# Attention scores on 32 rows a head: key columns without a block diagonal, and transposed scores with batch and key on partitions

## The reference

```python
q, k, v = proj(layernorm(x), Wq, bq), proj(ctx, Wk, bk), proj(ctx, Wv, bv)   # (B, 16, 64, 8)
q, k = _rope(q), _rope(k)
scores = jnp.einsum('bhqd,bhkd->bhqk', q, k) / math.sqrt(hd)
scores = jnp.where(m == 0, NEG_INF, scores)
p_attn = jax.nn.softmax(scores, axis=-1)
x1 = x + tanh(g_xattn) * (merge_heads(einsum('bhqk,bhkd->bhqd', p_attn, v)) @ Wo.T + bo)
# then: every row goes through the one of 8 experts (128 -> 512 -> 128, gelu) that its router picks
out = x1 + tanh(g_ffn) * gate * expert(layernorm(x1))
```

## Time and profile before

| what | value |
|---|---|
| median of three runs | 288.04 us (286.25 to 291.29) |
| the profiled execution | 287.01 us, its span 285.2 us |
| busy over the span | PE 80%, PEld 68%, DVE 66%, POOL 63%, ACT 58% |
| matmul records | 3785 |
| mean granted clock of TensorE | 0.958 of full speed |

### The profile page before, as it was taken

The page is one execution under the profiler, slowest core; times in us unless marked ns, Lnnn a source line. Parts: engine busy times, 40 slices in busy tenths (PEclk is TensorE's granted clock), DMA queues, the critical chain, the costliest instruction groups (busy, mean ns, idle before and its releaser), DMA issues.

```text
span 285.2 us, 11006 instructions
## 1 busy us (share of the span) xinstructions
PE 229.3 (80%) x3785; PEld 193.4 (68%) x3785; DVE 189.1 (66%) x639; ACT 164.9 (58%) x482; POOL 180.3 (63%) x222
## 2 busy tenths in 40 slices
PE   1357888987988987789879896598789899999950
PEld 1245677765866765667768675376689799999950
DVE  4546778788798888988867868886575344444310
ACT  1236669696677886568865886436464344444410
POOL 5366757568467889467896686704877654555550
PEclk9999999999799999979996999979999999999995
DMA  7801466546543673314351221333143443110100
GB/s 216 230 15 28 102 148 169 143 103 144 144 129 79 171 177 67 105 32 126 67 150 37 42 48 34 76 85 86 45 143 91 123 119 79 50 33 24 39 21 0
DMA packets 58537, 26.53 MB, mean 93 GB/s; under 512 B 38608, under 2 KB 53989, under 8 KB 58484
## 3 DMA queue, kind: packets, MB, share of 16 engines
q1 hardware_dynamic: 55204, 20.02, 29.3%
q0 software_dynamic: 2272, 4.46, 4.7%
q10 hardware_dynamic: 1008, 1.35, 1.6%
HBM read 16.57 MB, written 5.51 MB: 77 GB/s over the span
## 4 chain that ended last, share of the span: by engine, by line
PE 43%; DVE 19%; issue 11%; ACT 10%; POOL 5%; DMA 5%; SPq 3%; DVEq 0%; POOLq 0%
PE ps L752 13%; DVE mx L1240 5%; PE ps L771 4%; PE ps L795 4%; PE ps L770 3%; PE ps L733 3%; PE ps L735 3%; PE ps L734 3%; ACT vx L644 2%; DVE qk L1185 2%; SPq L411 2%; ACT kT L630 2%; DMA w_r<-in_W_last_row 2%; ACT qk L616 2%; DMA kbd<-kT 2%
## 5 line engine op out<-in xcount | busy, mean ns | idle before, releaser
L565 POOL DMA_INDIRECT out<-fin,got x39 | 37.9, 971 | 28.2 <-DVE fin L1299 23.4
L1240 DVE TENSOR_REDUCE mx<-ps 128x16 f16<-128x1024 f32 x32 | 39.0, 1219 | 12.8 <-PE ps L813 12.7
L752 PE MATMUL ps<-w_f,hT 128*128 x312 | 44.6, 286 | 0.1
L517 POOL DMA_INDIRECT rows<-x_all,dest_i x32 | 33.3, 1041 | 17.0 <-DVE x_all L1075 9.5
L795 PE MATMUL ps<-vx,pr 128*64 128x32 f32 x1024 | 38.0, 229 | 4.9 <-DVE on L1175 4.0
L795 PEld LDWEIGHTS ps<-vx,pr 128*64 128x64 f32 x1024 | 34.5, 144 | 8.9 <-issue 5.3
L544 POOL TENSOR_TENSOR rot<-qk,cf 128x256 f32<-128x256 f32 x32 | 23.4, 732 | 24.7 <-ACT qk L616 17.6
L752 PEld LDWEIGHTS ps<-w_f,hT 128*128 128x128 f32 x312 | 37.8, 191 | 1.1 <-issue 0.3
L1299 DVE SCALAR_TENSOR_TENSOR fin<-ps,got 128x128 f32<-128x128 f32 x39 | 13.7, 351 | 35.9 <-PE ps L752 35.9
L531 POOL TENSOR_TENSOR stk<-rot,stk 128x256 f16<-128x256 f32 x32 | 21.5, 671 | 20.4 <-DVE stk L1253 20.4
L594 ACT ACTIVATE pr<-ps 128x1024 f32<-128x1024 f32 x32 | 32.7, 1021 | 2.2 <-PE ps L843 1.6
(11 more groups left out here) (158 smaller groups left out, 585.1 us busy)
## 6 DMA issues: line engine op xcount, KB each, us to landing
kbd<-kT SPq DMA_DIRECT2D x128, 32.0 KB, 2.5
got<-rows SPq DMA_DIRECT2D x39, 72.0 KB, 2.0
w_f<-in_W_rows SPq DMA_DIRECT2D x8, 256.0 KB, 2.9
w_r<-in_W_last_row SPq DMA_DIRECT2D x8, 256.0 KB, 3.2
w_f<-in_L_ffn_W SPq DMA_DIRECT2D x8, 256.0 KB, 4.7
x_all<-in_x SPq DMA_DIRECT2D x3, 512.0 KB, 5.2
xt_all<-in_x_t SPq DMA_DIRECT2D x3, 512.0 KB, 4.8
ct_all<-in_ctx SPq DMA_DIRECT2D x3, 512.0 KB, 4.5
```

The costliest lines, as they stand in the source:

```text
L517: pool.indirect_dma_start(out=rows, out_offset=bass.IndirectOffsetOnAxis(ap=dest_i[:, t:t + 1], axis=0), in_=x_all[:, t, :], in_offset=Non ...
L565: pool.indirect_dma_start(out=out_d, out_offset=bass.IndirectOffsetOnAxis(ap=got_i[:, u % GOT, R_ID:R_ID + 1], axis=0), in_=fin[:, u % FRI ...
L752: mm = pe.matmul(o, hT[:, par, c, :], w2_f[:, bass.ds(e, 1), c, :].rearrange("p o n -> p (o n)"), start=False, stop=(c == FC - 1))
L1240: dve.tensor_reduce(mx[:, t % 2, :].rearrange("p (w h) -> p w h", w=2)[:, :, 0:8], ps_s[:, :].rearrange("p (w h k) -> p w h k", w=2, k=S), ...
```

## The change

`kbd` is gone, with its DMAs, its zeroing and its waits. `kT` gets four buffers. Scores are made for each head alone: 32 partitions, 64 query columns as weights, 64 keys moving, 32 products a tile. The transposed scores now have batch and key (64 + 64) on partitions and head by query in columns; each batch and head has one selector product and one product of kT and qT, 32 and 32 a tile. The value products take one head each: 32 fp32 products a tile (of 64 partitions, 64 columns as weights, 9 moving). The values lie in `vx` with batch and key on partitions, so that one ScalarE instruction copies them. Scores and transposed scores are made in two halves, in turn, each half with row blocks w and w + 2 (which write to different PSUM banks); each second half waits for the last product of the first one. Both stand after L825 in the step. SyncE issues the chunk and expert loads in one list. The exponential, the maximum and the copies of kT and qT keep their sizes.

```diff
-        kT = sb("kT", [P, 2, NA, P], F16)
+        kT = sb("kT", [P, RING, NA, P], F16)
-        kbd = sb("kbd", [P, RING, 2 * NA, 2, S], F16)
-        vx = sb("vx", [P, RING, 2, 8, 32])
+        vx = sb("vx", [P, RING, H, 16])
-        pr = sb("pr", [P, 2, 8, 2, S])
+        pr = sb("pr", [P, 2, H, S])
...
# SyncE
-            def step(i):
-                t = i - 1
-                if live(t):
-                    sp.wait_ge(kT_ev, t + 1)
...
-                    for g in range(4):
-                        r = slice(STK * g, STK * g + STK)
-                        sp.dma_start(kbd[r, s, :, g % 2, :],
-                                     kT[r, par, :, :].rearrange("p a (b k) -> p (a b) k", b=2)).then_inc(kbd_ld[s], 16)
...
+            columns_of(2)
+            context_of(2)
+            sp.dma_start(ids[:, :], const_i).then_inc(s_ids, 16)
+            expert_of(0)
+            columns_of(3)
...
+            for e in range(2, NE):
+                expert_of(e)
# GpSimd
-            pool.memset(vx[:, :, :, :, :], 0.0).then_inc(s_vz, 1)
-            pool.memset(kbd[:, 0:2, :, :, :], 0.0).then_inc(s_kz, 1)
# ScalarE
-                    if t >= 2:
-                        act.wait_ge(kbd_ld[(t - 2) % RING], ((t - 2) // RING + 1) * 64)
...
-                    for b in range(2):
-                        for hh in range(2):
-                            act.activation(vx[64 * hh:64 * hh + 64, s, b, :, 16 * hh:16 * hh + HD],
-                                           v_ps[64 * b:64 * b + 64, :, hh, :], ACT.Copy).then_inc(v_ev, 1)
+                    act.activation(vx[:, s, :, 0:HD], ps_kv[:, D:2 * D].rearrange("p (h d) -> p h d", d=HD), ACT.Copy
+                                   ).then_inc(v_ev, 1)
# TensorE
+            def scores(t, half):
+                s = t % RING
+                for a in range(NA):
+                    for b in range(2):
+                        for w in (half, half + 2):
+                            r, c = head_rows(w), (NA * w + a) * S
+                            mm = pe.matmul(ps_s[S * b:S * b + S, c:c + S], qT[r, s, a, S * b:S * b + S],
+                                           kT[r, s, a, S * b:S * b + S], start=True, stop=True)
+                return mm
+            def scores_T(t, half):
+                s = t % RING
+                for a in range(NA):
+                    for b in range(2):
+                        for w in (half, half + 2):
+                            r, c, k = head_rows(w), (NA * w + a) * S, slice(S * b, S * b + S)
+                            pe.matmul(ps_st[k, c:c + S], sel_h[r, a, :], mxT[r, t % 2, k], start=True, stop=False)
+                    for b in range(2):
+                        for w in (half, half + 2):
+                            r, c, k = head_rows(w), (NA * w + a) * S, slice(S * b, S * b + S)
+                            mm = pe.matmul(ps_st[k, c:c + S], kT[r, s, a, k], qT[r, s, a, k], start=False, stop=True)
+                return mm
...
-                    for j in range(8):
+                    for h in range(H):
                         for b in range(2):
-                            mm = pe.matmul(ps_o[S * b:S * b + S, 32 * j:32 * j + 32], pr[:, par, NA * (j % 2) + j // 2, b, :],
-                                           vx[:, s, b, j, :],
-                                           start=True, stop=True)
+                            k = slice(S * b, S * b + S)
+                            mm = pe.matmul(ps_o[k, 16 * h:16 * h + HD + 1], pr[k, par, NA * (h % 4) + h // 4, :],
+                                           vx[k, s, h, 0:HD + 1], start=True, stop=True)
...
-                    for a in range(NA):
-                        for b in range(2):
-                            for w in range(2):
-                                r, c = rows_half(w), (NA * w + a) * P
-                                mm = pe.matmul(ps_s[S * b:S * b + S, c:c + P], qT[r, s, a, S * b:S * b + S],
-                                               kbd[r, s, 2 * a + b, :, :].rearrange("p h k -> p (h k)"),
-                                               start=True, stop=True)
-                    mm.then_inc(s_done, 1)
# after the transpose of on (L825):
+                t = i - 2
+                if live(t):
+                    pe.wait_ge(kT_ev, t + 1)
+                    pe.wait_ge(qT_ev, t + 1)
+                    wait(pe, mx_done, t)
+                    scores(t, 0).then_inc(half_done, 1)
                 t = i - 3
                 if live(t):
...
+                    scores_T(t, 0).then_inc(st_half, 1)
+                t = i - 2
+                if live(t):
+                    pe.wait_ge(half_done, t + 1)
+                    scores(t, 1).then_inc(s_done, 1)
+                t = i - 3
+                if live(t):
+                    pe.wait_ge(st_half, t + 1)
+                    scores_T(t, 1).then_inc(st_done, 1)
# VectorE
-            dve.memset(kbd[:, 2:RING, :, :, :], 0.0).then_inc(s_kz2, 1)
...
-            for hh in range(2):
-                dve.memset(vx[64 * hh:64 * hh + 64, :, :, :, 16 * hh + HD:16 * hh + HD + 1], 1.0).then_inc(s_v1, 1)
+            dve.memset(vx[:, :, :, HD:HD + 1], 1.0).then_inc(s_v1, 1)
```

## The result

The changed kernel takes 362.2 us (median of four runs, 356.0 to 367.2) against 288.1 for the kernel before. The direction was right; the size was not. The forecast was 326, its range ended at 352, and what happened is rival B, the falling clock, which stood at 18%.

A forecast was written before the change was run, and what follows sets the result against it. A ring of waits through TensorE, VectorE and GpSimd bounds the ordinary step. Ordinary steps +25.6, heavy +6, tail +4.8, fourth and fifth +2.2, two value blocks +1.9, start −2: +38.5 on 285.2, forecast 326 us; range 304 to 352.

The forecast's parts named there:

- rival B: Attention steps: the clock falls; 356 to 380 us if in half of the steps, 340 in a fifth; chance 18%.
- Value block: TensorE's value products of a tile (L795 before): 32 products instead of 16, +0.94 us a tile, near 1.85 us.
- pair pace: Time per pair of value-product records, one for each batch half: 0.058 us, set by weight loads and kept after the change.
- Ordinary step: Attention step without routing on VectorE: 4.77 + 0.94 + 0.26 + 0.40 = 6.37 us, +1.60.
- score part: Scores and transposed scores on TensorE: 0.60 us from first to last start, +0.40; bounds 0.45 to 0.93.
- lengthens the step at full price: Work added on TensorE between L785's start and the maximum's start, 2.06 us before, adds its whole time to the step.
- Heavy steps: Ten attention steps in which VectorE also does routing: about 6.6 us instead of 6.04, +6 in all.
- The sum at full clock: All terms over the run together: +38.5 us, 285.2 becomes 323.7.
- The fourth and fifth steps: Early attention steps, counted apart from the ordinary and heavy ones: +2.2 us together.
- The last three: Tail attention steps, where VectorE's routing stands behind the maximum: +4.8 us together.
- The start: Before the steady steps: cheaper value copies and no first key wait, −2 us.
- ring of waits: Ordinary step: L813, maximum, stack copies, GpSimd's L531, L785 and value products wait on one another in turn, 4.77 us.

The follow-up runs named there:

- split kernel: The kernel before with each value product made twice, 16 of its 32 columns at a time, still on 128 rows: 314.1 us, ratio 1.084.
- 32-column kernel: The changed kernel with 32 moving columns in each value product instead of 9: 344.3 us, ratio 1.191.
- 64-column kernel: The changed kernel with 64 moving columns in each value product instead of 9: 331.4 us, ratio 1.148.

## Why the prediction was right in its structure and wrong in its size

- **Value block.** Forecast +0.94 at a pair pace of 0.058; 0.92 in the split kernel, 0.90 in the changed one at full clock. Right, and the reason given fits: neither rows (128 or 64) nor moving columns (9 to 64) change it. That the load sets the pace is the reading that is left; no run varied the load's columns. A weight load costs by its columns and not by its rows, as the Trainium skill says in "TensorE: Matmul & The Clock Gate", section LDWEIGHTS. As to the rows the traces agree (1.98 on 128 rows, 1.99 on 64).
- **Ordinary step.** Forecast 6.37, measured 6.08 with the clock up (32 columns; 6.11 with 64). Two terms were too large. The score part from L814 to the maximum's start was put at 1.13 and is 1.03 in the 32-column kernel. And the +1.60 was added in full to 4.77, while some 0.2 of it fell under the second branch, GpSimd's rotation into the stack copy, which I hadn't traced though its times stood in the same step. So "lengthens the step at full price" was wrong for the first 0.2.
- **Heavy steps.** Forecast 6.6. In the 64-column kernel most lie between 6.4 and 7.4, where data waits, stalls without a releaser and low stretches mix; the term was some tenths too small, and offsets the one above.
- **The sum at full clock.** +38.5 against +43 in the 64-column kernel looks close, and part of that is luck. In its profiled execution (335.6 us) the 25 steps between the fifth and the last three grew by 32.8 us, 31.6 forecast for 26 ordinary and heavy ones together, but with 7.6 us of stalls that no term had. The fourth and fifth steps grew by 4.8, 2.2 forecast (5.4 in the changed kernel), since the fourth runs at the low level, where the block priced at 1.85 takes 3.5. The last three grew by 7.9, 4.8 forecast. The start gave none of the 2 us forecast: the first maximum begins at 22.7 in both kernels.
- **A slip in the range.** The score part's bounds were said to move the ordinary steps by −4 or +9; that is for 26 steps, and the 16 ordinary ones give −2.4 or +5.3.
- **Waits.** All 32 maxima wait for the scores, about 2 us each; TensorE idles 0.53 ahead of L859 where the clock is up, 0.5 forecast. In the low steps that idle time shrinks or goes.
- **Feed-forward stage.** From the last maximum to the end it is 97.4 us before and 102.2 after, 1.9 forecast for two value blocks; the rest of it goes with the clock, 0.88 instead of 0.96 there. Of the span's growth 69 of 74 us lie in the attention stage.
- **The step that failed** is the weight given to rival B. The prediction priced it (half of the steps: 356 to 380; the result is 362) and named its cause, few rows and columns of the array at work, beside an idle time. That the price fits is partly luck: nine steps are low nearly throughout and cost 2.8 to 3.1 more than the 6.08 of full clock, inside the 2 to 3.6 forecast, but fifteen others alternate and cost 0.6 to 0.9. The prediction then set it at 18% with the sentence that TensorE is issued something nearly all the time. What the runs showed in its place: continuous issue doesn't keep the clock up when each product moves few columns. With the same products, 9, 32 and 64 moving columns gave 0.68, 0.82 and 0.94, at a busy share of 96%, 90% and 86%. The range ended at 352 because the upper half of B was left out, and that is where the time fell.
- **What stays open.** What the clock answers to over a whole step. How rows and columns weigh together is not settled. Products of 128 rows and 16 columns held 0.95 in the kernel before, and those of 64 rows and 32 columns held 0.82 in the changed one, but the two kernels differ in their scores and in their idle time too. Idle time may have its part: with the values last in the kernel before, the clock was 0.82 with full 32-column products, beside waits of TensorE of up to 1.4 us, 31.0 in all, in 23 steps. And with fp16 values the block is short and the clock lower still. The effects were not priced separately. Nor did I find a version that is faster than the kernel before by 2%; the nearest is its fp16 form, 0.9% faster with rounded values.

## What to carry to other kernels

Splitting a product to avoid multiplying zeros saves nothing when neither its rows nor its moving columns set its pace, and each half pays that pace again: here twice the products cost twice the block, whatever arithmetic was removed. Before you trust a sum made at full clock, ask how much streams in each product: a TensorE that is always issued something was still granted half its clock here, and that slowed down all the dense work beside the thin part. And before adding a cost to a ring of waits, trace what releases each of its links second to last; here that branch hid 0.23 of a loss of 0.92.

## What the runs showed of the hardware

- Granted clock over the attention stage, same products, value products with 9, 32, 64 moving columns: 0.68, 0.82, 0.94; on 128 rows with 9 and 16 columns: 0.84 and 0.95 (over the span, in four executions each, 0.867 to 0.907 and 0.907 to 0.933). TensorE's busy share in the first three was 96%, 90%, 86%. A high busy share did not go with a high clock.
- The same with the value products in fp16 instead of fp32, with half the records: 0.59 instead of 0.68 in the changed kernel, 0.88 instead of 0.95 in the one before.
- In the steps that alternate, the low level (1.2 GHz) falls on the stretch with large products that follows the thin one, not on the thin one itself (0.51 and 0.99 in turn).
- A product on fp32 with a 64-column load keeps a pace of some 0.03 us a record at full clock from 9 to 64 moving columns, on 64 rows as on 128. In fp16 it has half the records, and its block took 0.95 instead of some 3.5 us at the low clock.
- Filler in the idle time raised the clock from 0.68 to 0.80 and the median time gained nothing that the runs can tell (359.7 and 362.2 us): 14 products took 1.70 us at the low clock where 0.94 was meant.
- TensorE stalled without a releaser for up to about 1 us (1.03 in the row above) at full clock; with 64 columns 7.6 us in 14 places, with 32 columns and filler 13.1 in 21, before 2.4 in 4.
- At the start of a trace the clock column reads 1.00 while eight transposes take 1.06 us instead of 0.61.
